# Second attention with its tokens on the rows, and a last feed-forward layer whose packed weights are loaded a stage ahead, unpacked piece by piece and turned by DMA

## The reference, cut to what matters

```python
# second attention (L1): 16 query heads, 4 key/value heads, head size 96, keys = context tokens and x tokens (256)
q, k, v = heads(xn @ Wq.T), kv_heads(cat(ctx, xn) @ Wk.T), kv_heads(cat(ctx, xn) @ Wv.T)
x += merge(softmax(q @ k.T * 96**-0.5) @ v) @ Wo.T
# last feed-forward layer (L3), hidden size 1376; w1, w3, w2 are stored as int words that hold two 4-bit numbers
g = concatenate([w >> 4, (w & 15 ^ 8) - 8], axis=1).reshape(-1, 64)
W = (g.astype(float32) * s[:, None]).reshape(out_features, in_features)
x += (silu(xn @ W1.T) * (xn @ W3.T)) @ W2.T
```

## Time and profile before

| | us |
|---|---|
| median of 3 runs | 1761.84 |
| lowest and highest | 1760.46, 1802.96 |
| the profiled execution | 1778.61 |
| its span in the profile | 1777.1 |

### The profile page before, as it was taken

How to read it: one execution, slowest core, us unless ns; L and a number is a source line. 1 busy time by engine, 2 the same in 40 slices (tenths; PEclk the granted TensorE clock), 3 DMA queues, 4 the chain that set the end, 5 groups by cost and what they waited for, 6 DMA issues and landing times. The chain is left out here.

```text
span 1777.1 us, 30122 instructions
## 1 busy us (share of the span) xinstructions
PE 1566.7 (88%) x10596; PEld 891.3 (50%) x10596; DVE 1104.3 (62%) x2097; ACT 730.6 (41%) x2417; POOL 656.4 (37%) x618
## 2 busy tenths in 40 slices
PE   6999579997999999876999999999986588449997
PEld 5665234445666666433655555555542244324443
DVE  7665555535555555645888878878777798951211
ACT  4443345223443433223766666666543121441111
POOL 6684553000533434401766656656640000310000
PEclk8575679998999999987999999999998699779998
DMA  8695554102433323203755576554342000200001
GB/s 205 120 149 94 102 137 98 24 10 75 97 74 71 78 48 60 64 23 108 147 128 117 104 134 107 111 131 105 75 79 88 0 1 1 75 24 0 0 0 47
DMA packets 378460, 138.08 MB, mean 78 GB/s; under 512 B 336993, under 2 KB 362017, under 8 KB 378194
## 3 DMA queue, kind: packets, MB, share of 16 engines
q1 hardware_dynamic: 378322, 136.28, 35.7%
HBM read 52.87 MB, written 2.10 MB: 31 GB/s over the span
## 5 line engine op out<-in xcount | busy, mean ns | idle before, releaser
L1199 POOL TENSOR_TENSOR a_recip<-a_total,minus_one 128x4 f32<-128x4 f32 x96 | 98.0, 1021 | 196.0 <-ACT a_probs L1051 196.0
L1191 POOL TENSOR_TENSOR a_q_ss<-a_q_ss,half 128x4 f32<-128x4 f32 x64 | 89.3, 1395 | 189.6 <-DVE a_q_ss L1121 96.1
L1206 POOL TENSOR_TENSOR a_normal<-a_probs,a_recip 128x512 f32<-128x512 f32 x128 | 155.2, 1223 | 7.9 <-DMA a_p_t<-a_p_nat 0.5
L67 PE MATMUL bank<-a_wo_hi,a_o_hi 128*128 128x512 f16 (+1 forms) x384 | 145.5, 379 | 8.4 <-DVE x_state L1112 8.4
L69 PE MATMUL bank<-a_wo_hi,a_o_lo 128*128 128x512 f16 (+1 forms) x384 | 145.5, 379 | 0.0
L68 PE MATMUL bank<-a_wo_lo,a_o_hi 128*128 128x512 f16 (+1 forms) x384 | 145.5, 379 | 0.0
L1051 ACT ACTIVATE a_probs<-a_masked,a_negmax 128x128 f32<-128x128 f32 x256 | 99.5, 390 | 94.9 <-DVE a_negmax L1096 94.9
L1062 ACT ACTIVATE a_o_hi<-bank 128x512 f16<-128x512 f32 (+1 forms) x96 | 57.1, 595 | 180.6 <-PE bank L69 180.5
L67 PE MATMUL bank<-xn_hi,f_w_hi 128*128 (+2 forms) x288 | 111.2, 386 | 6.4 <-PEq L1267 5.3
L68 PE MATMUL bank<-xn_lo,f_w_hi 128*128 (+2 forms) x288 | 110.9, 385 | 0.0
L69 PE MATMUL bank<-xn_hi,f_w_lo 128*128 (+2 forms) x288 | 110.9, 385 | 0.0
(11 more groups left out here) (348 smaller groups left out, 4801.2 us busy)
## 6 DMA issues: line engine op xcount, KB each, us to landing
a_no<-in_L_xattn_Wo SPq DMA_DIRECT2D x9, 1024.0 KB, 6.0
a_nq<-in_L_xattn_Wq SPq DMA_DIRECT2D x8, 1024.0 KB, 5.5
...
```

Source lines behind the costliest of these rows:

```text
L67: pe.matmul(out, lh, rh, start=start, stop=False)
L1191: pool.tensor_tensor(r[:, :], r[:, :], K.half[:, 0:n], ALU.pow).then_inc(root_done.sem, 1)
L1199: pool.tensor_tensor(recip[s % 2][:, :], total[s % 2][:, :], K.minus_one[:, :], ALU.pow).then_inc(recip_done.sem, 1)
L1206: m = pool.tensor_tensor(normal[s % 2][:, t, :, :], probs[s % 2][:, :, t * P:(t + 1) * P], by, ALU.mult)
```

## The change

**Second attention** becomes `second_attention`. Queries, keys and values all come out with tokens on the rows (stationary operand: the tokens; moving: 384 columns of Wq, or 96 of Wk or Wv). Queries and keys are then split and turned by transposing transfers, and the layernorm rows too (two transfers a batch, `turn_rows`). The values carry one more column of ones, so that the mix (24 matmuls of 97 columns, stationary: the turned probabilities) gives the sum of the exponentials as well; the division is done on its result by DVE (`divide`), which is turned again by a transfer (`turn_heads`) and projected out in 3 x 3 matmuls of 512 columns. A step has 4 transposing transfers: queries (8 blocks), keys (4), probabilities (16), heads (6).

**Last layers.** `PackedWeights` holds words and scales of all three matrices in buffers of their own; SP loads them in stage 6 (10 transfers, 160 counts), after POOL has cleared the rows past the last tile. `streamed_packed_ffn` runs half-steps t from -10; tile u (22 of them) is at t = 2u. The matrices are cut into 33 pieces of at most 512 columns: per piece DVE shifts twice and later subtracts (`unpack`, `low_of_weight`), ACT converts and takes the high half (`to_float`, `high_of_weight`), POOL scales (`scale_weight`), SP turns it by a transfer (8 blocks; w2 in 8 transfers of 11 blocks at t = 2). Pieces of w1 and w3 for tile f come at half-step 2f - 10, those of w2 between -9 and 1; 20 pieces stand ahead of half-step 0. The down matmuls of a tile come 5 tiles later. Rows are normalised in two halves and turned by transfers.

```diff
+def second_attention(K, wq, wk, wv, wo):
...
+    G, H, D, KTL, W = 4, 4, 96, 2, 128
+    VW, OT = D + 1, H * D // P
+    TOTAL = G * B
+    by_q, by_w = float(D) ** -0.5 / WS, 1.0 / WS
+    NORM, KV, QUERY = -6, -3, -2
+    MIX, DIVIDE, OUT, ADD = 2, 2, 4, 4
+    WKV, WQ, WO, LOADO = -10, -4, -3, -6
+    PROBS, PN, PT, QT, KVB, XB = 3, 2, 5, 6, 6, 4
+    FIRST, END = min(NORM, WKV, WQ), TOTAL + ADD + 1
+    W_AT = {("kv", 0): WKV, ("wq", 0): WQ, ("wq", 1): WQ, **{("wo", i): WO + i for i in range(OT)}}
...
+        s_bank, o_bank = take("s", K.bank[0:3], units), take("o", K.bank[3:5], all_steps)
+        ring, y_bank = take("made", K.bank[5:7], made), take("y", K.bank[7:8], all_steps)
...
+                def turn_rows(b):
+                    sp.wait_ge(xlo_done.sem, xlo_done.count(b))
+                    for a, dst in enumerate((K.xn_hi, K.xn_lo)):
+                        sp.dma_start_transpose(dst[:, :, b * P:(b + 1) * P], xn_hl[b % XB][:, a, :]).then_inc(xt_in[b], 16)
...
+                def turn_probs(s):
+                    sp.wait_ge(plo_done.sem, plo_done.count((s, 1)))
+                    if s >= PT:
+                        mixed(sp, s - PT)
+                    sp.dma_start_transpose(p_t[s % PT][:, :, :, :, :].rearrange("p a h t n -> p (a h t) n"),
+                                           p_hl[s % PN][:, :, :, :].rearrange("p a t n -> p (a t n)")).then_inc(p_in[s % PT], 16)
...
+                load("kv", 0)
+                load("wq", 0)
+                for t in steps:
+                    for u in live(t - QUERY):
+                        turn_queries(u)
+                    if t == LOADO:
+                        load("wo", 0)
+                    for u in live(t - KV):
+                        turn_keys(u)
+                    for u in live(t):
+                        turn_probs(u)
+                    for b in first_group(t - NORM):
+                        turn_rows(b)
+                    for u in live(t - DIVIDE):
+                        turn_heads(u)
+                    for use in weights_at(t):
+                        kind, g, i = use
+                        if use == [u for u in pieces if u[:2] == (kind, g)][-1] and g + 1 < G:
+                            sp.wait_ge(wlo_done.sem, wlo_done.count(use))
+                            load(kind, g + 1)
...
+                def mix(s):
+                    landed(pe, p_in, s)
+                    split(pe, ("kv", s))
+                    pe.wait_ge(o_bank.freed(s), o_bank.n_free(s))
+                    for h in range(H):
+                        for t in range(KTL):
+                            m = pair_matmul(pe, o_bank[s][:, h * VW:(h + 1) * VW], tuple(p_t[s % PT][:, a, h, t, :] for a in range(2)),
+                                            tuple(v_hl[s % KVB][:, a, t, :] for a in range(2)), t == 0, t == KTL - 1)
...
+                for t in steps:
+                    for u in live(t - KV):
+                        keys_values(u)
+                    for u in live(t):
+                        scores(u, 0)
+                    for u in live(t):
+                        scores(u, 1)
+                    for u in live(t - QUERY):
+                        queries(u)
+                    for u in live(t - MIX):
+                        mix(u)
+                    for u in live(t - OUT):
+                        project_out(u)
...
+                for t in steps:
+                    for u in live(t):
+                        maxima(u, 0)
+                    for u in live(t):
+                        maxima(u, 1)
+                    for b in first_group(t - NORM):
+                        normalise(b)
+                    for use in weights_at(t):
+                        low_of_weight(use)
+                    for u in live(t - KV):
+                        low_of_keys_values(u)
+                    for u in live(t):
+                        high_of_probs(u, 0)
+                    for u in live(t - QUERY):
+                        low_of_queries(u)
+                    for u in live(t - DIVIDE):
+                        divide(u)
+                    for u in live(t):
+                        high_of_probs(u, 1)
+                    for u in live(t - ADD):
+                        add_to_x(u)
...
-def lag_attention(K, S):
+def lag_attention(K, S, packed):
...
+            @block.sync
+            def _(sp):
+                packed.load(sp)
...
+                packed.clear(pool)
...
+def streamed_packed_ffn(K, W):
...
+    CHUNK = 4
+    CHUNKS = -(-W2G // CHUNK)
+    NORM1, STATS2, NORM2 = -7, 5, 6
+    NORM = {b: NORM1 + b // 2 if b < HALF else NORM2 + 2 * (b - HALF) for b in range(B)}
+    START, LEAD = -10, 1
+    W2 = {n: START + LEAD + 2 * (n // 2) for n in range(CHUNKS)}
+    W13 = {f: START + (f if f < LEAD else 2 * f - LEAD + 1) for f in range(NT)}
+    SCALE, HIGH, LOW, TURN = 0, 2, 2, 1
+    LAG, HB, IB, FB, XN, XB = 5, 3, 3, 4, 2, 4
...
+                for t in steps:
+                    for b in at(NORM, t):
+                        turn_rows(b)
+                    if t == max(W2.values()) + TURN:
+                        sp.wait_ge(wlo_done.sem, wlo_done.count(("w2", CHUNKS - 1)))
+                        for a in range(2):
+                            for k in range(PER):
+                                sp.dma_start_transpose(w2_t[:, a, :, k, :], w2_hl[:, a, k * HID:k * HID + NT * P]).then_inc(w2_in, 16)
+                    for use in pieces_at(t - TURN):
+                        if use[0] != "w2":
+                            turn_weight(use)
+
...
+                for t in steps:
+                    for u in live(t):
+                        into_hidden(u, "up", "w1")
+                        into_hidden(u, "gate", "w3")
+                    for u in live(t - 2 * LAG):
+                        down(u)
...
+                def to_float(use):
+                    i = slot(use)
+                    act.wait_ge(ints_done.sem, ints_done.count(use))
+                    if place[use] >= FB:
+                        act.wait_ge(wlo_done.sem, place[use] - FB + 1)
+                    act.activation(as_row(flat[i], use), as_row(ints[place[use] % IB], use), ACT.Copy, scale=WS).then_inc(float_done.sem, 1)
+
+                def high_of_weight(use):
+                    act.wait_ge(scaled_done.sem, scaled_done.count(use))
+                    if use[0] != "w2" and w13.index(use) >= FB:
+                        turned(act, w13[w13.index(use) - FB])
+                    act.activation(halves_of(use)[0], as_row(flat[slot(use)], use), ACT.Copy).then_inc(whi_done.sem, 1)
...
+                for t in steps:
+                    for u in live(t):
+                        silu(u)
+                    for use in pieces_at(t - HIGH):
+                        high_of_weight(use)
+                    for b in at(NORM, t):
+                        high_of_rows(b)
+                    for u in live(t):
+                        high_of_hidden(u)
+                    for use in pieces_at(t):
+                        to_float(use)
...
+                def unpack(use):
+                    m, f = use
+                    i, src = place[use] % IB, source(use)
+                    if place[use] >= IB:
+                        dve.wait_ge(float_done.sem, place[use] - IB + 1)
+                    n = groups_of(use)
+                    dve.tensor_scalar(ints[i][:, 0:n, 0, :], src, 4, None, ALU.arith_shift_right)
+                    dve.tensor_scalar(ints[i][:, 0:n, 1, :], src, 28, 28, ALU.logical_shift_left,
+                                      ALU.arith_shift_right).then_inc(ints_done.sem, 1)
+
+                def low_of_weight(use):
+                    hi, lo = halves_of(use)
+                    dve.wait_ge(whi_done.sem, whi_done.count(use))
+                    dve.tensor_tensor(lo, as_row(flat[slot(use)], use), hi, ALU.subtract).then_inc(wlo_done.sem, 1)
...
+                take_stats(0)
+                for t in steps:
+                    for use in pieces_at(t):
+                        unpack(use)
+                    for u in live(t - 2 * LAG - 2):
+                        if u % NT == NT - 1:
+                            for n in range(HALF):
+                                add_to_x(u // NT, n)
+                    for b in at(NORM, t):
+                        normalise(b)
+                    for u in live(t):
+                        gated(u)
+                    if t == STATS2:
+                        take_stats(1)
+                    for use in pieces_at(t - LOW):
+                        low_of_weight(use)
+                    for u in live(t):
+                        low_of_hidden(u)
+
...
+                def scale_weight(use):
+                    rows = as_groups(flat[slot(use)], use)
+                    pool.wait_ge(float_done.sem, float_done.count(use))
+                    pool.tensor_tensor(rows, rows, scale_of(use), ALU.mult).then_inc(scaled_done.sem, 1)
...
+                roots(0)
+                for t in steps:
```

(29 more changed lines are left out.)

683 lines of the change are left out of this document (525 added, 158 removed).

## The result

| | before | after |
|---|---|---|
| median beside each other (4 runs each), us | 1774.75 | 1700.76 |
| lowest and highest | 1760.46, 1802.96 | 1697.79, 1707.99 |
| the profiled execution | 1778.61 | 1702.35 |

The ratio of the two is 0.966, with an interval from 0.961 to 0.972; it leaves out runs more than 1.5% above the fastest of their kernel, so that of the kernel before only the two at 1760.46 and 1761.84 us count in it (the medians of all four give 0.958). Forecast were 1659 us and a range of 1636 to 1708: the range holds the time, the value itself was 42 us too low. Of those, 26.6 us are in the profile (1777.1 - 103 = 1674 forecast, 1700.6 measured), and 16.8 are the step from the profiled execution to the median of 1761.84, of which 1.6 come back because the profiled execution of after lies that much above its own median.

What follows compares the result with a forecast made beforehand. The second attention was taken as bound by PE, the last layer as a 76.6 us four-engine chain, then 181 us of PE. Gains 58 + 45 = 103 us, subtracted from the median 1761.84, gave 1659 us, range 1636 to 1708.

Steps and rivals of the forecast that it cites:

- PE's sum of a step: Second attention: matmuls of one step sum to 8.26 us instead of 10.1, 264.3 us in all, 59.2 less.
- The base: Whole kernel: the 103 us gain was subtracted from the median 1761.84 us, the profiled execution being 16.8 above it.
- Nothing waits in the steady part: Second attention: new waits reach PE two steps later only; transfers, 7.0 us a step, stay hidden.
- B: Second attention: transfers set the step, 9.8 us instead of 8.26, 48 us less gain, 1707 us; chance 0.15.
- E: Second attention: TensorE's clock stays at 1.2 GHz, a step costs 16.5 us, 1923 us in all; chance 0.06.
- The fill: Start of the second attention: 29 SP issues at 1.25 us take 36 us; batch 7 has landed at about 454.
- The tail: End of the second attention: two chains through a transfer, last mix and last out, about 4 us.
- Stage 6 at zero: Stage 6: loads hide in some 90 us and cost zero; without that cover, one load, 6 us.
- The last layer: Last layer: overlapping weight preparation with matmuls ends it at 1722 against 1767.5; gain 45 us, bounds 35 and 56.
- the w2 transfers: Last layer: eight transfers from half-step 2, issued until about 1575, in time for the first down matmul at 1584.
- POOL and DVE: Last layer's pieces: the two hold each other up, so taken as serial, 2.24 us a piece; other bound 1.24.
- rival C: Last layer: POOL and DVE hardly meet in the pieces, gain 56 instead of 45, 1648 us; chance 0.14.

Runs made afterwards that it cites:

- rows_one: Kernel after, with each batch's rows in the second attention turned by one transfer instead of two: stage 2 294.7 us, 5.2 less; ratio to before 0.951.
- best_first: Kernel combining all edits that shortened a stage, with second-attention rows normalised at step b - 11 instead of b - 6: stage 2 298.0 us against 294.5; ratio to before 0.946.
- late_spread: Kernel after, with stage 6 loads issued behind POOL's roots and w2 transfers sent two by two: stage 7 221.4 us instead of 225.7 and 226.3.
- scale_dve: Kernel after, with the last layer's product by the scales moved from POOL to DVE and ACT's conversion removed: stage 7 222.3 us, against 225.7 and 226.3.

## Why the forecast was 42 us too low

The mechanism of both changes was right: PE's sum of a step, nothing waiting in the steady part, and the overlap in the last layer. The steps that failed are terms of the sum. In the profile the 26.6 us are 13.6 in the second attention, 6.7 in stage 6, 4.3 in stage 3, 2.9 in the last layer, and 0.9 the other way in the rest. Ahead of them comes the base, 16.8 us of luck in the clock. The largest step of the gain that failed is the fill: SP's issue was priced at 1.25 us and took 1.52, and the lower clock was charged only to the first matmuls.

- **The base** (16.8 us). "Subtracted from the median": 1761.84 was a median of runs with a short stage 0. Compared with its own profile, the kernel was forecast at 1674 and came to 1700.6.
- **PE's sum of a step**: right, 8.30 against 8.26 us, with the interpolated price of 384 columns.
- **Nothing waits in the steady part**: right, and rivals B and E did not happen; the clock is at 1.00 from step 5 to step 28. That SP needs 5.0 us a step for its issues was wrong (7.0), and cost nothing.
- **The fill**: wrong. From the end of the stage ahead to the last matmul 285.6 us were forecast (691 - 405.4), and 299.9 came. 11.4 of these 14.3 us lie ahead of step 5: by the forecast PE had 220.8 of its 264.3 us left there and was done with them at 685, so step 5 began at 464.2, 58.8 us after the stage ahead; it began at 70.2. The first matmul came 1.7 us later than before's (9.2 us, behind the weights' split on DVE), PE waited 10.8 us and lost 5.7 to the lower clock, where the forecast had 7.8 for both; these are 10.4 of the 11.4. The terms that failed are the issue at 1.25 us (1.52) and its landing at 2.5 (4.0), and the clock, which I charged only for the first matmuls; rows_one gave back 5.2 of them. The median of 1.29 us in the earlier trace rows was a mixture of two stages; the second attention alone had 1.60. What sets the other 6 us was not isolated; turning the rows earlier did not bring them back (best_first).
- **The tail**: 5.4 us of waits and 1.4 of lower clock instead of 4, nearly all of the other 3 us.
- **Stage 6 at zero**: wrong, 2.9 us through POOL's late roots. I looked for who waits for the loads, not for what they delay. Of the other 3.8 us there 2.9, and of the 4.3 in stage 3 3.9, are the clock's scatter, of which the forecast knew nothing.
- **The last layer**: right in mechanism, 42.1 for 45. The first pair matmul came 32.6 us after the stage ahead, where the forecast had 31.7 (1541 less 1509.3); from the first to the last matmul 182 us for 183. Inside, sizes were off and cancelled by luck: a piece is 1.85 us, not 2.24; the third tile waited 1.1 us, not the 4 to 5 forecast, because ACT reached half-step 0 43.5 us after the first statistics, not 47; but the w2 transfers, "in time", were not: 8 issues took 14.6 us, the last landed at 1548, PE waited 2.4 and ran at the lower clock after it. late_spread showed that at 4.3 to 4.9 us. A wait of 2.1 us inside tile 5, for DVE, was not forecast either.
- **POOL and DVE**: shifts stretched from 0.28 to 1.13 us, as forecast, and rival C fell. The Trainium skill's rule (SBUF — State Buffer, Who interferes with whom) agrees with that: beside POOL's product the shifts take four times as long, and in scale_dve, where POOL has no product, none is stretched before the first matmul.
